# A fused block of two cross-attentions, a quantised feed-forward and an expert layer: loads in smaller pieces, two memsets elsewhere, and all five queues in another order

## The reference

```python
x = x + xattn0(layernorm(x), ctx, mask0)     # q, k, v, scores / sqrt(8), mask, softmax, @ v, @ Wo.T
x = x + ffn0(layernorm(x))                   # act_quant(x) @ weight_quant(w_gate), silu, * up, quant, @ w_down
x = x + xattn1(layernorm(x), ctx, mask1)     # per-head 8x8 weights, one mask for all batches
x = x + moe(layernorm(x))                    # h = relu(x @ W1[e].T + b1), y = h @ W2[e].T + b2, top 2 of 8
# ffn0: weight_quant takes the mean of |w| over each weight; act_quant takes the row's maximum of |x|
```

## Time and profile before

| | |
|---|---|
| timed runs | 214.77, 214.84, 215.25 us (median 214.84) |
| the profiled execution's own time | 216.64 us |
| its span, first to last instruction | 214.8 us |
| PE busy | 196.6 us, 92% |
| DVE busy | 162.4 us, 76% |
| ACT busy | 135.3 us, 63% |
| POOL busy | 82.7 us, 38% |
| mean granted TensorE clock | 0.987 of 2.4 GHz |

### The profile page before, as it was taken

The page is one execution under the profiler, slowest core; times in us unless marked ns, Lnnn a source line. Parts: engine busy times, 40 slices in busy tenths (PEclk is TensorE's granted clock), DMA queues, the critical chain, the costliest instruction groups (busy, mean ns, idle before and its releaser), DMA issues.

```text
span 214.8 us, 6119 instructions
## 1 busy us (share of the span) xinstructions
PE 196.6 (92%) x2114; PEld 160.8 (75%) x2114; DVE 162.4 (76%) x608; ACT 135.3 (63%) x378; POOL 82.7 (38%) x197
## 2 busy tenths in 40 slices
PE   2487697999999999999999999999999999999992
PEld 0255474757766777777888988898979889999992
DVE  6458989999999999999987859966576736265225
ACT  3343466468868677766968579547955576566430
POOL 4494320432337544143520425438210604232532
PEclk9999889999999999999999999999999999999998
DMA  5849678504440724430080000400220000000000
GB/s 156 243 111 303 164 98 349 145 9 101 108 92 0 160 50 92 98 87 17 2 92 9 5 0 17 98 3 12 54 47 6 0 15 0 17 0 15 2 10 24
DMA packets 39747, 15.09 MB, mean 70 GB/s; under 512 B 34211, under 2 KB 38819, under 8 KB 39462
## 3 DMA queue, kind: packets, MB, share of 16 engines
q1 hardware_dynamic: 39142, 14.00, 27.7%
q10 hardware_dynamic: 576, 0.72, 1.0%
HBM read 5.80 MB, written 0.52 MB: 29 GB/s over the span
## 4 chain that ended last, share of the span: by engine, by line
PE 81%; DVE 7%; DMA 5%; issue 2%; SPq 2%; POOL 1%; ACT 1%; DVEq 0%; ACTq 0%
PE ps_B L826 14%; PE ps_A L839 12%; PE ps_O L756 7%; PE ps_B L690 7%; PE ps_A L675 6%; PE ps_B L692 6%; PE ps_Q L708 6%; PE ps_A L677 6%; DMA m0T_i<-in_mask0T 5%; PE ps_O L764 3%; PE ps_X L722 2%; PE ps_A L791 2%; PE ps_O L774 2%; PE ps_A L835 2%; PE ps_P L736 2%
## 5 line engine op out<-in xcount | busy, mean ns | idle before, releaser
L907 ACT ACTIVATE probs<-ps_B 128x512 f32<-128x512 f32 x64 | 36.5, 598 | 15.6 <-PE ps_B L692 14.8
L956 ACT ACTIVATE hid<-ps_B,b_sb 128x128 f32<-128x128 f32 x128 | 35.6, 378 | 15.3 <-PE ps_B L826 15.2
L1063 DVE TENSOR_REDUCE mx<-ps_A 128x4 f32<-128x512 f32 x64 | 42.0, 677 | 3.7 <-PE ps_A L677 3.7
L826 PE MATMUL ps_B<-mxT,w_sb 128*128 128x128 f32 x256 | 33.3, 278 | 0.0
L839 PEld LDWEIGHTS ps_A<-w_sb,hid 128*128 128x128 f32 x256 | 31.1, 192 | 0.6
L839 PE MATMUL ps_A<-w_sb,hid 128*128 128x128 f32 x256 | 31.2, 275 | 0.0
L826 PEld LDWEIGHTS ps_B<-mxT,w_sb 128*128 128x128 f32 x256 | 30.6, 192 | 0.5 <-issue 0.4
L654 POOL TENSOR_TENSOR yc<-yc 128x512 f32<-128x512 f32 (+2 forms) x21 | 17.3, 823 | 34.1 <-DVE yc L1228 33.0
L675 PE MATMUL ps_A<-m_b,id_b 128*128 128x512 bf16 x64 | 24.7, 385 | 2.4 <-DVE mx L1063 1.2
L692 PEld LDWEIGHTS ps_B<-qmT,kblk 118*128 118x128 bf16 x256 | 20.4, 100 | 8.6 <-issue 0.8
L692 PE MATMUL ps_B<-qmT,kblk 118*128 118x128 bf16 x256 | 25.5, 223 | 0.0
(11 more groups left out here) (135 smaller groups left out, 391.5 us busy)
## 6 DMA issues: line engine op xcount, KB each, us to landing
w_sb<-in_m1T SPq DMA_DIRECT2D x1, 1024.0 KB, 6.2
w_sb<-in_m2T SPq DMA_DIRECT2D x1, 1024.0 KB, 8.1
out_y<-out_sb SPq DMA_DIRECT2D x8, 64.0 KB, 1.5
x_sb<-in_x SPq DMA_DIRECT2D x1, 448.0 KB, 6.7
ctx_sb<-in_ctxT ACTq DMA_DIRECT2D x1, 448.0 KB, 5.5
m_i<-in_mask SPq DMA_DIRECT2D x1, 384.0 KB, 4.2
m0T_i<-in_mask0T SPq DMA_DIRECT2D x1, 384.0 KB, 5.0
kblk<-kst SPq DMA_TRANSPOSE x16, 3.7
```

Of the source, the lines that this page charges most:

```text
L826: mm = pe.matmul(psum("z", b, i)[:, c * P:(c + 1) * P], w1_sb[:, 4 * i + c, :], mxT[:, b % 2, :], start=True, stop=True)
L907: ends(act.activation(probs[:, n % 2, 4 * i:4 * i + 4, :], psum("exp", n, i)[:, :].rearrange("p (h k) -> p h k", h=4), ACT.Exp, scale=ATTN ...
L956: ins = act.activation(hid[:, b % 2, 4 * i + c, :], psum("z", b, i)[:, c * P:(c + 1) * P], ACT.Relu, bias=b1_sb[:, 4 * i + c:4 * i + c + 1])
L1063: ends(dve.tensor_reduce(mx[:, n % 2, 4 * i:4 * i + 4], psum("max", n, i)[:, :].rearrange("p (h k) -> p h k", h=4), AX.X, ALU.max), "dve.max")
```

## The change

It has four parts. First, loads in smaller pieces: x and ctx in batch 0, 1 to 3, 4 to 7; layer 0's masks in four parts (batch 0; 1; 2 and 3; 4 to 7); the experts' two weights in four parts each, behind the transposes of units 3 to 6; layer 1's loads one transpose later. Second, the memset of the second kst buffer goes from VectorE to POOL, that of bank ps_O goes behind VectorE's first `rk`, and POOL's memsets of ones and rows3 go behind the keys of unit 0 (`late_constants`). Third, `TIME` and `ARRIVES` have new numbers, `START` has six numbers for each unit (one for each group of steps in `STAGES`), `BIAS` is new throughout, and units (1,1) and (0,6) change places. Fourth, some tiles share memory (yc with the two bias tiles, th and hr with the weights before quantisation); the counts of buffers stay 3, 2 and 2, now by name. No instruction of the computation is added or removed. SP issues 35 loads before the stores, where it issued 23.

```diff
+QSLOTS = 3
+TSLOTS = 2
+MSLOTS = 2
+MASK_PART = {0: 0, 1: 1, 2: 2, 4: 3}
-UNIT_ORDER = ((0, 0), (0, 1), (0, 2), (0, 3), (0, 4), (0, 5), (1, 0), (1, 1), (0, 6), (0, 7), (1, 2),
+UNIT_ORDER = ((0, 0), (0, 1), (0, 2), (0, 3), (0, 4), (0, 5), (1, 0), (0, 6), (1, 1), (0, 7), (1, 2),
 TIME = {
-    "pool.km": (0.53, 0.56), "pool.kl": (0.42, 0.49), "sp.ks": (2.5, 4.5), "pe.xT": (0.12, 0.32),
+    "pool.km": (0.53, 0.56), "pool.kl": (0.42, 0.48), "sp.ks": (1.7, 4), "pe.xT": (0.22, 0.34),
...
-LATENCY = 0.1
+LATENCY = 0.04
-START = (-52, -44, 20, 12, 22, 133, 38, 67, 117, 100, 152, 77, 98, 83, 149, 113)
+START = ((-4, -571, -962, -105, -628, -2279), (2, -41, -494, -422, -188, -436),
...
+STAGES = ("dve.st dve.ag pool.pw dve.nm pe.xT act.xT pe.q act.qh dve.rq pool.qm pool.ql pe.qs act.qs sp.qs pool.xb",
+          "pe.kv act.kh act.v dve.rk pool.km pool.kl sp.ks",
...
+GROUP = {name: k for k, names in enumerate(STAGES) for name in names.split()}
-                queues.setdefault(name, []).append((n, i, before, START[n] + depth + BIAS[l].get(name, 0.0)))
+                queues.setdefault(name, []).append((n, i, before, START[n][GROUP.get(name, 5)] + depth + BIAS[l].get(name, 0.0)))
-            sp.dma_start(x_sb[:, 1:NB, :], x[1:NB].rearrange("b t d -> t b d")).then_inc(s_x, 16)
+            sp.dma_start(x_sb[:, 1:4, :], x[1:4].rearrange("b t d -> t b d")).then_inc(s_x, 16)
                 if n == 0:
+                    masks(1, 1, 2)
                     sp.dma_start(wo_sb[0][:, :], w0o).then_inc(s_wo, 16)
+                    sp.dma_start(x_sb[:, 4:NB, :], x[4:NB].rearrange("b t d -> t b d")).then_inc(s_x4, 16)
+                    sp.dma_start(ctx_sb[:, 4:NB, :], ctxT[:, 4:NB, :]).then_inc(s_ctx4, 16)
                 if n == 1:
-                    masks(1, 2, NB)
+                    masks(2, 2, 4)
                     for k, src in enumerate((wg, wu, wd)):
                         sp.dma_start(wf_sb[:, k, :], src).then_inc(s_wf[k], 16)
                 if n == 2:
+                    masks(3, 4, NB)
+                if n == 3:
                     sp.dma_start(m1_i[:, :], mask1).then_inc(s_mask1[0], 16)
...
-                    sp.dma_start(w1_sb[:, :, :], m1T).then_inc(s_moe, 16)
-                    sp.dma_start(w2_sb[:, :, :], m2T).then_inc(s_moe, 16)
+                if n in (3, 4, 5, 6):
+                    part = slice(4 * (n - 3), 4 * (n - 3) + 4)
+                    sp.dma_start(w1_sb[:, part, :], m1T[:, part, :]).then_inc(s_moe, 16)
+                    sp.dma_start(w2_sb[:, part, :], m2T[:, part, :]).then_inc(s_moe, 16)
-            masks(0, 0, 2)
+            masks(0, 0, 1)
@@ POOL
-            pool.memset(ones[:, :], 1.0).then_inc(ones_ready, 1)
-            pool.memset(rows3[:, :], 0.0).then_inc(small_ready, 1)
+            zeros(kst[:, 1, :, :, :]).then_inc(small_ready, 1)
             def late_constants():
+                pool.memset(ones[:, :], 1.0).then_inc(ones_ready, 1)
+                pool.memset(rows3[:, :], 0.0).then_inc(small_ready, 1)
                 pool.memset(b2_p[:, :], 0.0).then_inc(b2_zero, 1)
@@ ACT
-            act.dma_start(ctx_sb[:, 1:NB, :], ctxT[:, 1:NB, :]).then_inc(s_ctx, 16)
+            act.dma_start(ctx_sb[:, 1:4, :], ctxT[:, 1:4, :]).then_inc(s_ctx, 16)
@@ DVE
-            zeros(kst[:, 1, :, :, :]).then_inc(kst_zero, 1)
-            dve.memset(banks["O"][0][:, :], 0.0).then_inc(bank_zero, 1)
+                    if n == 0:
+                        dve.memset(banks["O"][0][:, :], 0.0).then_inc(bank_zero, 1)
```

177 lines of the change are left out of this document (93 added, 84 removed), and 7 rows, old and new, of the table START.

## The result

The changed kernel takes 221.74 us (median of four runs, 221.48 to 223.23), the kernel before 214.84 (214.77 to 215.25): ratio 1.033, 95% interval 1.028 to 1.038. It is 6.9 us slower, where 2.1 us faster was forecast and 215.5 was the range's end.

A forecast was written before the change was run, and what follows sets the result against it. VectorE was taken to bound the kernel until about 100 us, TensorE after. Terms +0.9 - 1.2 - 1.5 - 0.3 = -2.1 from 214.84 gave 212.7 us, range 209.6 to 215.5.

The forecast's parts named there:

- Part 1: Front until the first reduction: qr's 2.3 us gain is lost on POOL and TensorE; +0.9 us (0 to +1.7).
- Part 2: 15 to 20 us: VectorE's mask wait goes, eight reductions of units 0 and 1 fill in; -1.2 us (0 to -1.3).
- Part 3: 20 to 40 us: reductions and weight steps cover the reciprocal's wait and small score waits; -1.5 us (0 to -1.6).
- Part 4: 40 to 100 us: half of VectorE's remaining 0.65 us idle time is won; -0.3 us (+1.5 to -0.6).
- The premise: Before 100 us VectorE's queue counts: its gains are kept, those of TensorE alone are worth nothing.
- Part 5: Loads in pieces: 12 more on SP, some 6 us of its queue, with no reduction or matmul waiting for kblk; nothing.
- Part 6: After 100 us: TensorE is full, unit 14's keys just fit near the end by 1.0 us; 0 (0 to +1.5).
- Rival D: Slower, near the end: unit 10's late sum delays keys of 14 and 15, TensorE stands still; 215.3 to 217, 17 in 100.
- rival B: More is won, if the clock stays 2.4 GHz and matmuls are short by 14 us; 209.8 to 211.5, 22 in 100.
- C: Front's gain is given back: until 50 us each wait of VectorE or TensorE becomes the other's; 214.3 to 215.3, 11 in 100.
- the signs that were named: Trace marks: statistics 3.3, first reduction 15.2 to 16.9, no late mask or kblk waits, low VectorE idle, TensorE full near 98.
- the two of being wrong: VectorE idle over 1 us waiting for scores in 20 to 50 us, or TensorE under 99% busy after 100 us.

The follow-up runs named there:

- the second profile: The unchanged kernel before, profiled again: median 214.56 us, span 212.7 us, granted clock 1.00 throughout.
- the weights behind: Changed kernel with first unit let through, `wm` earlier, unit 5's key parts earlier, and feed-forward weights issued and reduced later, behind unit 2's transpose and first maximum: 222.83 us.
- the three repairs: Changed kernel with first unit let through, `wm` earlier on TensorE, and unit 5's kr and key parts ahead of queries of units 4 and 5: 220.75 us.
- letting the first unit through: Changed kernel with unit 0's query turn, query parts, first scores and first reductions put earlier on the queues: 221.28 us, first reduction at 13.54.

## Why the prediction was wrong

**The step that failed** is the pair of terms of parts 2 and 3, -1.2 and -1.5: the waits seen in one execution were booked as won, and the new order was given none of its own. Against the second profile these stages got 1.84 and 0.75 us more idle time instead of 2.7 less. With parts 1 and 4 (+0.93, +1.36) VectorE's idle time before 100 us rose by 4.9 us where -2.1 was forecast. The rule that the end follows VectorE's idle time fell short too: the span grew by 7.1.

**The rows it was read from.** Parts 2 and 3 took 2.7 us from 2.8 us of idle time between 15 and 40 us. Other profiles of the same code have 0.7, 0.9 and 1.7 there, so 1 to 2 us of the term were not to be had in most executions. The text saw that the profiled execution was 1.8 us above its median and moved only the starting point of the sum, not its terms.

**Part 1** was right in mechanism: the 2.3 us of qr were won (2.1) and lost on GpSimd and TensorE. The first reduction came at 16.47, inside 15.2 to 16.9, and idle time before 15 us grew by 0.93 for a term of +0.9.

**Part 2** failed. No mask is waited for any more, as forecast, but "Are the second unit's scores there?" asked after the wrong unit: with long matmuls the scores of unit 0 themselves come slower than VectorE reduces them (one part in 0.85 us, from 15.37 to 16.22, against 0.69 for a reduction), and the turn of unit 1 stands between them. The waits are 0.89, 0.16 and 0.75 us. The eight reductions were also counted at 0.6 us where the earlier trace rows has 0.69, and they end at 23.5 instead of 21.5. +1.84 instead of -1.2.

**Part 3** failed at "if nothing new is late". `wm` was, which stands behind pv of unit 0: VectorE waits 1.12 us for it, which is nearly all of its 1.16 us in 20 to 40. Moving `wm` gave 0.8 us of the end, within noise. TensorE met a new wait too, 0.88 us for unit 2's keys, and behind it in turn is unit 2's mask; VectorE had other work meanwhile. +0.75 instead of -1.5.

**Part 4** had the right bounds and the wrong side: +1.36 where +1.5 to -0.6 were given.

**The premise** that a microsecond TensorE alone gains before 100 us is worth nothing is not borne out: 0.8 us put in at 61 us came out as 0.8. TensorE's 3.2 us less in 40 to 100 us (55.30 against 58.53) had no term in the sum, because the prediction held them to be free.

**Part 5.** No reduction waits for a kblk landing, but one matmul does, at 24.02. SP needs 3.04, 4.53 and 3.13 us to issue the transposes of units 1 to 3, where the second profile of before has 1.33, 2.32 and 1.59. The end does not show it: with the new order and the old loads they take 1.33, 2.67 and 1.97, and the time is 220.97.

```profile
11.53 3.04 SPq L592 DMA_TRANSPOSE kblk<-kst  x1
...
17.25 4.53 SPq L592 DMA_TRANSPOSE kblk<-kst  x1
...
23.04 3.13 SPq L592 DMA_TRANSPOSE kblk<-kst  x1
```

**Part 6 and the rivals.** Rival D did not happen: after 150 us nobody waits for kblk, and TensorE is busy 109.64 of 110 us from 100 on. Of rival B's two conditions one came true, the granted clock of 1.00 (2.4 GHz) throughout the profiled execution; the other, short matmuls by 14 us, did not (eight transposes still take 1.06 us at 17.08), and neither did its gain. The Trainium skill, "TensorE: Matmul & The Clock Gate", section "Part 1: The HAM clock gate", says that activity lifts the clock. The trace agrees as far as it goes: TensorE was busy 5.00 of 5 us in 15 to 20, the eight transposes took 0.61 us at 19.49, and no drop followed. That the new order keeps the clock is not shown: five profiles with the old order have no drop either, and two with the new one have (0.83 in 30 to 40 us with `wm` early, 0.66 in 15 to 20 with the weights behind). C's mechanism, each queue's wait becoming the other's, fits the three repairs, which gave 1.0 of 2.0 us (0.45, 0.8 and the 0.73 of the wait at 53.0), though their intervals overlap; the loss on top is not in it.

Of the signs that were named, the two of being wrong did not come (0.2 us of waits for scores in 20 to 50, TensorE busy 99.7% after 100 us), so they would have let the miss pass; the one that caught it is VectorE's idle time from the first reduction to 40 us, 2.07 for "under 0.5".

What TensorE still has to do at 100 us shows how much of the loss was made by then. Its groups from 100 us on, in the changed kernel:

```profile
L858 PE MATMUL ps_B<-mxT,w_sb 128*128 128x128 f32 x256 | 33.4, 278 | 0.0
...
L707 PE MATMUL ps_A<-kblk,qT 112*128 112x256 bf16 x52 | 10.0, 272 | 0.0
L705 PE MATMUL ps_A<-m_b,id_b 128*128 128x512 bf16 x26 | 9.9, 381 | 0.0
...
L738 PE MATMUL ps_Q<-id_b,qst 128*118 128x128 bf16 (+1 forms) x104 | 8.1, 221 | 0.0
```

and in the second profile of the kernel before:

```profile
L826 PE MATMUL ps_B<-mxT,w_sb 128*128 128x128 f32 x256 | 33.3, 278 | 0.0
...
L708 PE MATMUL ps_Q<-id_b,qst 128*118 128x128 bf16 (+1 forms) x88 | 6.7, 219 | 0.0
...
L677 PE MATMUL ps_A<-kblk,qT 112*128 112x256 bf16 x40 | 7.7, 272 | 0.0
L675 PE MATMUL ps_A<-m_b,id_b 128*128 128x512 bf16 x20 | 7.6, 381 | 0.0
```

The experts are all still ahead in both (256 matmuls). The changed kernel has six parts of scores more to do (at 0.44 us, the pitch from 24.02 to 24.46 us in its timeline) and two turns (eight transposes each, 0.45): 3.5 us, and with the smaller groups (kv, q, gate, exp) about 5. So some 5 of the 7.1 us, an estimate from these counts and pitches, were lost by 100 us, on both engines alike. The other 2 came later, with no named wait of TensorE above 0.3 us in that stretch.

**What stays open.** The order as a whole is shown to cost 6.2 of the 6.9 us; which steps of it do is not. VectorE's idle time before 40 us rose by 3.5 us, yet letting the first unit through gave 0.45 and the old front in place of the new one 0.2, with a stall at its seam. The loss of TensorE between 60 and 100 us, nearly all of it between 60 and 80 (17.26 of 20 us against 19.50), goes with the new order of that stretch: busy 36.4 to 37.2 of 40 us in the eight kernels that have it, 38.7 to 39.5 in nine with the old. But the two that delay the old order by hand at 54 us and from 34 us on have 37.7 and 37.8, so a delay ahead of 60 us can look the same. Unit 0's late feed-forward is one candidate left, and the 2 us after 100 are unexplained.

## What to carry to other kernels

Before idle time of one profile is priced as a gain, compare that execution with the median and see the stretch in others: here four executions of one code had 0.7 to 2.8 us of "waits to win". An interleaved order that fills two engines to 98% may not bear being changed in part: the change and nine other orders tried here ended 2 to 4% behind the old one, while an edit of the front alone, ahead of the first reduction, where there was real idle time, won 0.3%. A new order has new waits; a forecast that prices only the removal of the old ones has no term for them. Price a delay at its own length or more on either of two coupled queues: 2.05 us put in cost 2.0 in the fastest execution and 3.1 in the median, 0.8 us cost 0.8. And measure in the trace what a delay put in by hand really took: seven transposes meant as 1.5 us were 0.8.

## What was not expected of the hardware

The issue of a transposing transfer kept SP from 1.3 to 5.1 us; it was long where loads had just been issued (4.53 us behind two masks and three weights of 256 KB, 1.33 us behind one weight of 64 KB three microseconds earlier). And the granted clock fell to half for 3.4 us in one of two profiles of the same kernel; TensorE had been busy 3.38 of the 5 us ahead of the fall (20 to 25) and 3.84 of the same 5 us in the profile without it. What such a fall goes with can be read from the executions of the kernel with seven transposes added: the ten with a mean clock of 0.996 or more took 215.1 to 215.6 us, the two at 0.992 216.8 and 216.9. The time before the first short matmuls is another thing: there the transposes take 1.06 us at a granted clock that is shown as 1.00.
